# Another order of blend, choice, copies and roots in a fractal mixer, and an earlier load of the experts' b2 rows

## The reference

```python
log_m = log(box_sums(x, 2, 4, 8, 16) + EPS)            # four scales
alphas = slope of log_m over log(scale)
excite = sigmoid(relu(mean(alphas) @ w1 + b1) @ w2 + b2)
sim = (a * b).sum(-1) / (norm(a) * norm(b) + EPS)      # a, b: centred log_m and its line
x = x * excite
mixer = sim * sigmoid(alpha_norm) + (1.0 - sim) * x
# experts of layer 0: top 1 of 8, capacity 1280; hidden 512
logits = t @ gate_w + gate_b
idx, prb = best of softmax(logits)
y = (relu(t @ w1[idx] + b1[idx]) @ w2[idx] + b2[idx]) * prb
```

## Time and profile before

| what | us |
|---|---|
| median of 3 runs (2357.2 to 2367.01) | 2364.84 |
| the profiled execution | 2363.5 |
| its span | 2361.8 |
| TensorE busy | 1751.2 (74%) |
| VectorE busy | 1549.3 (66%) |
| ScalarE busy | 1176.6 (50%) |
| GpSimd busy | 980.9 (42%) |

### The profile page before, as it was taken

One profiled execution on the slowest core, in us unless ns is written; L12 is line 12 of the kernel. 1 busy time (PEld: TensorE's weight loads), 2 busy tenths in 40 slices (PEclk: granted clock), 3 DMA queues, 4 the chain that ended last, 5 costly groups with the idle time before them and its releaser, 6 DMA issues. The chain is left out here.

```text
span 2361.8 us, 46309 instructions
## 1 busy us (share of the span) xinstructions
PE 1751.2 (74%) x10964; PEld 1380.4 (58%) x10981; DVE 1549.3 (66%) x4683; ACT 1176.6 (50%) x2637; POOL 980.9 (42%) x969
## 2 busy tenths in 40 slices
PE   1488665895388887989971477779918999988992
PEld 1133554895243443989971244657717777687992
DVE  6898686676677777635537677645665677754554
ACT  2445774895233332757752233446726444454661
POOL 0000133453004343655544066677740255466662
PEclk9799666998699999999995687789959999999996
DMA  2002002222201011232223112133343010123326
GB/s 73 1 0 69 16 25 55 55 77 88 82 2 35 22 33 54 64 85 69 68 75 115 36 46 75 60 89 104 90 142 109 19 34 31 50 70 97 92 78 218
DMA packets 183551, 153.81 MB, mean 65 GB/s; under 512 B 40290, under 2 KB 162818, under 8 KB 183358
## 3 DMA queue, kind: packets, MB, share of 16 engines
q1 hardware_dynamic: 153406, 92.37, 14.5%
q0 software_dynamic: 29952, 59.26, 7.4%
HBM read 85.33 MB, written 68.79 MB: 65 GB/s over the span
## 5 line engine op out<-in xcount | busy, mean ns | idle before, releaser
L1212 POOL DMA_INDIRECT returned<-rows_second_choice x488 | 481.8, 987 | 329.5 <-DVE rows_second_choice L1143 119.3
L1011 PE MATMUL psum<-rows_first_choice 128*128 128x128 f32 x3360 | 473.2, 282 | 19.1 <-ACT rows_first_choice L1060 14.7
L1021 PE MATMUL psum<-expert_weights,rows_first_choice 128*128 x2784 | 428.3, 290 | 61.6 <-ACT rows_first_choice L1077 21.8
L1011 PEld LDWEIGHTS psum<-rows_first_choice 128*128 128x128 f32 x3360 | 431.8, 199 | 21.1 <-issue 15.1
L1021 PEld LDWEIGHTS psum<-expert_weights,rows_first_choice 128*128 128x128 f32 x2784 | 362.8, 198 | 99.2 <-issue 93.0
L795 POOL DMA_INDIRECT dispatched<-rows_first_choice,slot x192 | 191.6, 998 | 525.2 <-DVE rows_second_choice L695 375.9
L1077 ACT ACTIVATE rows_first_choice<-psum,bias_columns 128x128 f32<-128x128 f32 x1104 | 323.4, 368 | 171.4 <-PE psum L1011 154.3
L795 POOL DMA_INDIRECT dispatched<-rows_second_choice,slot x192 | 191.5, 998 | 58.5 <-issue 58.2
L1118 DVE COPY rows_first_choice<-expert_weights 128x512 f32 (+1 forms) x272 | 105.5, 388 | 147.4 <-PE psum L1011 122.1
L326 PE MATMUL psum<-identity,rows_first_choice 128*128 128x128 f32 x256 | 41.2, 320 | 202.8 <-DVE rows_first_choice L313 190.8
L1143 DVE SCALAR_TENSOR_TENSOR rows_second_choice<-psum,rows_second_choice,rows_first_choice 128x128 f32<-128x128 f32 x344 | 119.4, 347 | 103.4 <-PE psum L1021 101.3
(11 more groups left out here) (369 smaller groups left out, 3272.9 us busy)
## 6 DMA issues: line engine op xcount, KB each, us to landing
rows_second_choice<-dispatched SPq DMA_DIRECT2D x488, 65.0 KB
expert_weights<-returned SPq DMA_DIRECT2D x12, 1024.0 KB, 10.4
rows_second_choice<-returned SPq DMA_DIRECT2D x8, 1024.0 KB, 10.7
returned<-rows_second_choice POOLq DMA_INDIRECT x488
expert_weights<-in_L_ffn_w SPq DMA_DIRECT2D x3, 2048.0 KB, 8.3
residual<-in_x SPq DMA_DIRECT2D x8, 512.0 KB, 7.2
rows_first_choice<-returned SPq DMA_DIRECT2D x4, 1024.0 KB, 8.9
out<-residual SPq DMA_DIRECT2D x8, 512.0 KB, 6.0
```

The lines of the kernel that those rows point to most:

```text
L1011: ins = pe.matmul(k.ps[:, self.PSH + u % 2, j * P:(j + 1) * P], self.wc[:, u % 2, j * P:(j + 1) * P], self.xt[:, u % 2, :], start=True, st ...
L1021: ins = pe.matmul(self.result_bank(u), self.gs[:, u % self.HB, j * P:(j + 1) * P], self.second[:, bass.ds(e, 1), j, :].rearrange("p a c -> ...
L1212: pool.indirect_dma_start(out=k.returned[0:N * self.K, :], out_offset=bass.IndirectOffsetOnAxis(ap=self.rt[:, u, C:C + 1].bitcast(I32), ax ...
```

## The change

It has three parts.

1. `Experts.sync` issues the b2 load right behind the first of the sixteen row loads, in layers 0, 1 and 2.
2. In the mixer's loop, VectorE blends before it chooses: the difference for the next image is computed ahead (`difference`), between choice and placing. TensorE does the late fold of image b before it ranks image b-1. ScalarE's `excite` is split from `gates` and moved ahead of `keep_rows`; `keep_sum` and `roots` of the next image come at the end of the round, ahead of the small root of this one. VectorE's wait for its own `mix_used` at the end of a round goes.
3. Ahead of the loop, TensorE no longer waits for the last squares before the squeeze matmuls; ScalarE excites image 0 while it waits for the energies, and does the gates of images 0 and 1 one after the other.

```diff
--- Experts.sync
-        for u in range(RING):
-            load(u, u)
+        load(0, 0)
         if self.b2 is not None:
             sp.dma_start(self.b2rows.rearrange("p e c -> p (e c)"),
                          self.b2.rearrange("e c -> (e c)").partition_broadcast(P)).then_inc(self.s["bias_rows"].h, 16)
+        for u in range(1, RING):
+            load(u, u)
--- Experts.tensor
-        route.turn_back(pe, B - 1)
+        if not route.folded:
+            route.turn_back(pe, B - 1)
--- mixer_fractal, vector
+            def difference(b):
+
+                dve.wait_ge(*when("mix_excited", b + 1))
+                dve.wait_ge(*when("mix_sig", 2 * b + 1))
+                if b:
+                    dve.wait_ge(*when("mix_used", b))
+                c2.note(dve.tensor_tensor(logs[:, 1, :], logs[:, 2 + b % 2, :], sqr[b % 2], ALU.subtract))
+
+            invert_norm(0)
             make_energy(B - 1)
             route.reset(dve)
-
+            difference(0)
             for b in range(B):
-                at, sig = energy[:, b, :], sqr[b % 2]
+                at = energy[:, b, :]
                 if b:
                     route.add(dve, b - 1)
                     route.invert(dve, b - 1)
-                    c2 = invert_norm(b)
+                    invert_norm(b)
                 dve.wait_ge(*when("mix_sig", 2 * b + 2))
-                c2.note(dve.tensor_tensor(at, slope[:, b, :], at, ALU.mult))
-                dve.wait_ge(*when("mix_excited", b + 1))
-                c2.link(dve.tensor_tensor(logs[:, 1, :], logs[:, 2 + b % 2, :], sig, ALU.subtract))
+                c2.link(dve.tensor_tensor(at, slope[:, b, :], at, ALU.mult))
+                dve.tensor_tensor(at, at, logs[:, 1, :], ALU.mult).then_inc(s["mix_used"].h, 1)
                 if b:
                     route.choose(dve, b - 1)
-                assert c2.n == BLEND
-                dve.tensor_tensor(at, at, logs[:, 1, :], ALU.mult).then_inc(s["mix_used"].h, 1)
+                if b + 1 < B:
+                    difference(b + 1)
                 if b:
                     route.place(dve, b - 1)
-                dve.wait_ge(*when("mix_used", b + 1))
--- mixer_fractal, scalar
+            excite(0)
             act.wait_ge(*when("mix_energy", 3 * B))
             gates(0)
-            for b in range(B):
-                if b:
-                    route.keep_sum(act, b - 1)
-                    route.root(act, b - 1)
-                    route.normalise(act, b - 1)
-                    route.keep_rows(act, b - 1)
+            gates(1)
+            excite(1)
+            roots(1)
+            route.keep_sum(act, 0)
+            for b in range(1, B):
+                route.root(act, b - 1)
+                route.normalise(act, b - 1)
                 if b + 1 < B:
+                    excite(b + 1)
+                route.keep_rows(act, b - 1)
+                if b + 1 < B:
+                    gates(b + 1)
+                route.exp(act, b - 1)
+                if b + 1 < B:
+                    route.keep_sum(act, b)
                     roots(b + 1)
-                    gates(b + 1)
-                if b:
-                    route.exp(act, b - 1)
             ex.scalar(act)
--- mixer_fractal, tensor
-            pe.wait_ge(*when("mix_squares", 5 * B))
+            pe.wait_ge(*when("mix_squares", 5 * (B - 1) + 3))
...
+            pe.wait_ge(*when("mix_squares", 5 * B))
             fold_early(pe, 0)
-            for b in range(B - 1):
+            for b in range(B):
                 route.turn_back(pe, b)
-                fold_early(pe, b + 1)
-                route.turn_rows(pe, b)
-                route.gate(pe, b)
-                route.rank(pe, b)
+                if b:
+                    route.rank(pe, b - 1)
+                if b + 1 < B:
+                    fold_early(pe, b + 1)
+                    route.turn_rows(pe, b)
+                    route.gate(pe, b)
             ex.tensor(pe)
```

More of the change, by code:

```diff
@@ L1429, in _ @@
             dve.tensor_scalar(sq[:], sums[:], slope_scale / IMG, None, ALU.mult).then_inc(s["mix_prep"].h, 1)
-            BLEND = 3
+            c2 = Chain(dve, s["mix_sim"], s["mix_sim"].base + B)
             def invert_norm(b):
-                c2 = Chain(dve, s["mix_sim"], s["mix_sim"].base + B + b * BLEND)
                 dve.wait_ge(*when("mix_root", 2 * b + 2))
                 c2.link(dve.reciprocal(energy[:, b, :], energy[:, b, :]))
-                return c2
-            c2 = invert_norm(0)
+            def difference(b):
[5 more added lines that the diff above has]
+            invert_norm(0)
             make_energy(B - 1)
             route.reset(dve)
+            difference(0)
             for b in range(B):
-                at, sig = energy[:, b, :], sqr[b % 2]
+                at = energy[:, b, :]
                 if b:
@@ L1526, in gates, with excite @@
                 act.activation(slope[:, b, :], slope[:, b, :], ACT.Square, scale=norm_scale).then_inc(s["mix_sig"].h, 1)
+            def excite(b):
                 if b >= 2:
```

## The result

The changed kernel took 2337.31 us (median of 4 runs, 2335.11 to 2339.93), the kernel before, on the same chip, 2363.63 (4 runs): ratio 0.9892, 95% interval 0.9868 to 0.9916, 26.3 us less. The forecast was 2342 and 22.4 us less. The profiled execution took 2337.0 us with a span of 2335.2, against 2363.5 with 2361.8. Later, in another group of runs, the same file took 2335.23 against 2359.22, ratio 0.9894 (0.9872 to 0.9915). The medians are of all runs, the ratio leaves out one far slower run on either side.

A forecast was written before the change was run, and what follows sets the result against it. Engines taking turns in the blending stretch, then a wait for b2, bound the start of the experts. First tile 20.4 us earlier (13.5 b2, 6.9 loop and entry) plus 2.0 in layer 1 gives 22.4 less: 2342, range 2337 to 2347.

The forecast's parts named there:

- Part 1: Layer 0's first expert tile: b2 load issued ahead of fifteen row loads, 13.5 us of the earlier start.
- R: Blending loop: start of VectorE's long reciprocal, once per image, from which the forecast counts its times; image 7's forecast at 372.0.
- (b): Layer 0's first expert matmul: VectorE's two copies of turned rows behind placing image 6 come last, R+17.7, that is 389.7.
- Rival D: Row loads: b2's 512 KB ahead of them brings the second tile's rows up to 4.6 us later; 2346, chance 0.05.
- Part 2: Blending loop, one image in the new order: 20.3 us against 21.07, 0.8 less per image, 4.6 over six.
- The cover of the roots: ScalarE in the blending loop: the next image's roots, now ahead of the small root, have 1.2 us of cover.
- Rival S: ScalarE's queue: the next image's roots hold up the small root VectorE waits for; slower, 2377, chance 0.02.
- Part 3: Entry into the blending loop: ScalarE free and first fold done earlier, gain 2.3 us, bounds 0 and 2.4.
- Part 4: Layers 1 and 2: the early b2 load gains 2.0 us in layer 1, between 0 and 2.4, and 0 in layer 2.
- The clock: TensorE in the blending loop: the late fold behind the gate matmuls starts at the half clock, 3.78 us.
- Rival W: Blending loop: clock up by the gate matmuls' end, fold 1.95 us, 19.0 per image, about 2334; chance 0.12.
- Rival L: Blending loop unchanged, layer 1 gives back its 2 us; only b2 and half the entry count, 2350; chance 0.16.

The follow-up runs named there:

- x2: Changed kernel with the b2 load back behind the sixteenth row load; ratio to the kernel before 0.992 (0.9891 to 0.9949).
- x3: Changed kernel with the early b2 load in layer 0 alone, late in layers 1 and 2; ratio to the kernel before 0.9887 (0.9857 to 0.9916).
- x8: The kernel before, unchanged, profiled again in a later group; one run, 2357.4 us.
- x9: The changed kernel, unchanged, run again in a later group; 2335.23 us, ratio to the kernel before 0.9894 (0.9872 to 0.9915).
- x5: Changed kernel with the ranking of image b-1 put back ahead of image b's late fold on TensorE; ratio to the kernel before 0.990 (0.9867 to 0.9932).
- x7: Changed kernel with six unread 0.6 us copies behind each image's roots on ScalarE; ratio to the kernel before 0.9901 (0.9867 to 0.9934).
- x6: Changed kernel with the entry into the blending loop as it was before; ratio to the kernel before 0.989 (0.9859 to 0.9921).
- x12: Changed kernel with nine useless 512-column matmuls per image in TensorE's gaps (six, one, two); ratio to the kernel before 0.986 (0.983 to 0.9891).
- x10: Changed kernel with seven useless 512-column matmuls per image in TensorE's gaps (five, one, one); 2332.08 us, ratio to the kernel before 0.9884.
- x1: Kernel before with only the b2 load moved ahead of fifteen row loads, layers 0 to 2; ratio to the kernel before 0.9979 (0.9957 to 1.000).
- x11: Changed kernel with five useless 512-column matmuls per image, all behind the early fold; 2332.58 us, ratio to the kernel before 0.9877.
- x4: Changed kernel with 27 useless 128-column matmuls per image in TensorE's gaps; ratio to the kernel before 0.9945 (0.9925 to 0.9965).

## Why the prediction was right, step by step

- **Part 1, b2.** 13.5 us forecast of the 20.4 at the first tile; 14.6 between x2 and x3, 14.1 between the two first traces, 14.9 between x8 and x9. The mechanism is as written: the load goes out 0.4 us behind the first row load (the working had 1.1) and the wait is gone. The row loads began at 379.25, 3.5 us before the 382.7 of the working, since image 6's R came at 349.49 and not 352.1; so b2 was less close to being last than it said.
- **What is late next.** Forecast (b), VectorE's copy behind placing, at R+17.7; it was VectorE's copy (L1126), and the matmul began at 388.36 = R+17.1. Rival D had no place to act: TensorE began by VectorE's copy, not by a late row load.
- **Part 2, the beat.** 20.3 forecast, 20.28 and 20.25 measured, but made up differently, so that the close agreement is partly luck: five beats of 19.6 to 20.1 and a last one of 21.8 (21.4 in x9). In the last image VectorE also lays out the plan (some 1.7 us between placing and statistics, 366.20 to 367.89), which the old order hid in VectorE's waits and the new one does not. The walk for a single image was thus 0.2 us too long, and the plan was missing in it. The gain per image against before depends on which trace of before one takes: 0.8 from 21.07, 0.6 from x8's 20.83, where more of the transposes were warm (beats of 20.5, four of six in x8 and two of six in the first trace). The working took the average of 21.07 without this. x5 shows that the step that makes the gain is the fold's place ahead of the ranking, 0.8 us per image over the loop.
- **The cover of the roots.** 1.2 forecast, 1.08 idle in the rows, 1.2 to 1.3 by x7. Rival S was rightly low.
- **Part 3, the entry.** 2.3 forecast with 2.4 as the upper bound; 2.95, 2.9 and 3.0 measured (first traces, x8 to x9, x6). Of the first two 0.4 and 0.3 were there ahead of the edited rows, at 222 us, which leaves 2.6. The bound failed, by little: the sum's copy itself gained 2.9 (248.10 to 245.21), or 2.65 against x6. One table load (1.28) and one copy (1.13) had been priced; ScalarE's busy stretch also starts 0.2 us earlier than in x6. The rest is small steps between operations that I had not counted.
- **Part 4, layer 1.** 2.0 forecast. The third tile came 1.8 earlier relative to the first, as said (1.9); the stage got 3.1 and 2.9 us shorter (284.6 to 281.5, 284.8 to 281.9), over the bound of 2.4. Which later wait gave the last microsecond wasn't tried apart, and x3, meant to try the load of layer 1 by itself, met no wait on it: this part is read from two pairs of traces, not shown by an experiment. In layer 2 the stage was 2.2 shorter in one pair and 1.3 longer in the other: nothing, as forecast.
- **The clock.** The forecast kept the cold fold, and it stayed cold: 3.76 in six of the seven images of the loop, 3.37 in the first (259.44). Rival W had it wrong that gate matmuls and fold back to back would raise the clock by themselves. Its price, 19.0 for a warm fold behind cold transposes and gate, no run tried; the working's bound for VectorE alone, 18.1, is what x12 reached with all three warm.
- **Rival L** falls by the beat, which did get shorter (20.28 from 21.07), and by x2: the order alone gives 6.0 to 7.0 us at the first expert matmul.
- **What begins earlier ends earlier.** The working took the experts as a fixed length. Of the 21.7 us at their start 19.9 were there at the end of layer 0, and 21.2 and 23.3 between x8 and x9. For the change the step held within 2 us; x10's 5.9 us were not kept.
- **Sum.** 26.5 against 22.4 between the profiled executions. At the first expert matmul 21.7 against 20.4, of which 0.65 is the entry's excess and 0.6 the first tile's; layer 1 1.1 more. The remaining 1.7 lie between and behind the stages, where pairs of traces differ by 1 to 2 us in either direction, and have no cause shown.

## What to carry to other kernels

Where engines take turns, walk one round from a fixed operation and ask for each queue what stands ahead of an operation that is already fit to run: here an independent fold stood behind a ranking that had to wait, and moving it was worth 0.8 us per image over the loop, while busy times stayed within 3 us. Compare the same rounds with each other, and look at the last and the first separately, since extra work hidden in an old wait comes out when the wait goes. A load that the whole first tile needs belongs ahead of loads for later tiles, and what that is worth is the distance to the next wait, not the length of the wait removed.

## What the runs showed of the hardware

- Gate matmuls of 8 columns kept TensorE busy for 3.58 us at clock 0.50 and the clock did not rise until 3.76 us of fold behind them were done: 0.50 from 275.6 to 282.6, 1.00 from 282.9. With useless matmuls of 512 columns in the gaps (x12) the granted clock was 0.91 to 1.00 over whole beats in place of 0.66. Where it fell there, it fell behind the gate matmuls with TensorE busy throughout: 3.30 of 3.30 us from 294.4 to 297.7, at 0.58.
- The same kernel took 2359 and 2634 to 2671 us in different groups of runs at nearly the same mean clock (0.87 to 0.88 in the profiles of before and changed, 0.84 to 0.86 in those of the long groups). The slow group's traces hold waits that the profile puts down as remote. The longest groups in x1 (engine, line, waited for: us in total, times, longest):

```profile
DVE logits L651 <- remote: 78.4, 8, 15.1
ACT rows_first_choice L1078 <- remote: 73.5, 10, 13.1
ACT turned_rows L781 <- remote: 72.1, 11, 9.3
```

  In all of x1 they add up to 184 us on VectorE and 220 on ScalarE, partly at the same time; the traces of before, changed and x8 to x11 have none. All three are waits for results of TensorE whose matmuls the records show as done. What holds TensorE's signal back there is open.
- x4's 27 extra matmuls per image met such a wait in five images of the loop, x12's nine wide ones in none, in a group that has them elsewhere. Whether it is the number of instructions was not tried apart.
